# A mixture-of-experts kernel whose W1 is loaded in four column slices

## What is computed

```
t = h.reshape(B * S, -1)
probs = softmax(t @ W_gate + b_gate)
topv, topi = top_k(probs, 2)            # shares normalized to 1
mid = relu(einsum('nd,edh->neh', t, W1) + b1)     # W1: 8 x 256 x 1024
eout = einsum('neh,ehd->ned', mid, W2) + b2       # W2: 8 x 1024 x 256
out = einsum('ne,ned->nd', route, eout) @ W_out + b_out
return x + out
```

## Time and profile before

| | us |
|---|---|
| median of 3 runs | 515.55 |
| lowest, highest | 514.03, 515.56 |
| the profiled execution | 515.1 |
| its span, first to last instruction | 513.2 |
| PE busy | 494.9 |
| DVE busy | 380.6 |
| ACT busy | 283.2 |
| POOL busy | 217.5 |

### The profile page before, as it was taken

The page is one execution under the profiler, slowest core; times in us unless marked ns, Lnnn a source line. Parts: engine busy times, 40 slices in busy tenths (PEclk is TensorE's granted clock), DMA queues, the critical chain, the costliest instruction groups (busy, mean ns, idle before and its releaser), DMA issues.

```text
span 513.2 us, 14538 instructions
## 1 busy us (share of the span) xinstructions
PE 494.9 (96%) x4658; PEld 430.7 (84%) x4659; DVE 380.6 (74%) x742; ACT 283.2 (55%) x576; POOL 217.5 (42%) x264
## 2 busy tenths in 40 slices
PE   7889998899999999999999999999899999999997
PEld 7556687788888888888888888889799999998786
DVE  4789987677786776878768787676568887864675
ACT  3533544655666556665566665336668778780221
POOL 4500025048456384464844637435545453321121
PEclk9999999999999999999999999999999999999999
DMA  6406534846556464555645543433354445133983
GB/s 225 158 2 209 190 125 124 237 143 205 139 172 188 140 213 131 164 179 155 198 144 163 175 122 93 115 100 99 91 163 150 135 130 150 34 114 126 406 333 140
DMA packets 75812, 80.62 MB, mean 157 GB/s; under 512 B 42983, under 2 KB 61740, under 8 KB 74732
## 3 DMA queue, kind: packets, MB, share of 16 engines
q1 hardware_dynamic: 56912, 41.44, 26.2%
q0 software_dynamic: 7936, 22.29, 13.0%
q10 hardware_dynamic: 10908, 16.17, 9.9%
HBM read 53.40 MB, written 26.48 MB: 156 GB/s over the span
## 4 chain that ended last, share of the span: by engine, by line
PE 83%; DMA 5%; issue 5%; DVE 3%; ACT 2%; ACTq 1%; SPq 0%; another core or an unknown queue 0%; DVEq 0%
PE bank L1399 24%; PE bank L1386 10%; PE bank L1325 8%; PE bank L1326 7%; PE bank L1327 7%; PE bank L1218 5%; PE bank L1455 5%; PE bank L1372 4%; PE bank L1374 4%; PE bank L1373 4%; DMA gq<-rows_by_slot 2%; DMA w1s<-y_by_choice 1%; PE bank L1465 1%; PE bank L1188 1%; DMA brow<-in_L_ffn_b_in 1%
## 5 line engine op out<-in xcount | busy, mean ns | idle before, releaser
L713 ACT ACTIVATE region<-bank,b1p,cbits 128x256 f32<-128x256 f32 (+1 forms) x368 | 163.1, 522 | 131.9 <-PE bank L1327 51.7
L567 POOL DMA_INDIRECT y_by_choice<-region,dst x71 | 87.3, 1229 | 166.9 <-DVE region L1063 151.5
L1399 PE MATMUL bank<-w2s,region 128*128 x1200 | 136.0, 273 | 0.9 <-issue 0.7
L1399 PEld LDWEIGHTS bank<-w2s,region 128*128 128x128 f16 x1200 | 116.7, 98 | 16.7 <-issue 2.9
L1094 DVE TENSOR_TENSOR region<-region 128x512 f16<-128x512 f32 (+1 forms) x184 | 104.0, 575 | 27.7 <-ACT region L697 20.4
L1325 PE MATMUL bank<-region,w1s 128*128 128x256 f16 x384 | 104.7, 273 | 4.3 <-DVE region L1100 2.2
L1327 PE MATMUL bank<-region,w1s 128*128 128x256 f16 x384 | 104.7, 273 | 0.0
L1326 PE MATMUL bank<-region,w1s 128*128 128x256 f16 x384 | 104.7, 273 | 0.0
L559 POOL DMA_INDIRECT region<-z_by_token,src x71 | 71.9, 1013 | 75.4 <-DVE src L1020 50.6
L1090 DVE CAST region<-region 128x512 f16<-128x512 f32 x100 | 46.0, 460 | 52.1 <-ACT region L713 47.9
L1372 PE MATMUL bank<-region 128*128 128x128 f16 x336 | 57.5, 219 | 1.1 <-DVE region L1100 0.5
(11 more groups left out here) (267 smaller groups left out, 644.4 us busy)
## 6 DMA issues: line engine op xcount, KB each, us to landing
region<-in_L_ffn_W ACTq DMA_DIRECT2D x14, 1024.0 KB
rows_by_slot<-region SPq DMA_DIRECT2D x33, 256.0 KB
gq<-rows_by_slot SPq DMA_DIRECT2D x132, 64.0 KB
w1s<-y_by_choice SPq DMA_DIRECT2D x12, 512.0 KB, 11.1
w1s<-in_x SPq DMA_DIRECT2D x8, 512.0 KB, 8.3
z_by_token<-w1s SPq DMA_DIRECT2D x16, 256.0 KB, 2.1
region<-in_L_ffn_W SPq DMA_DIRECT2D x2, 1024.0 KB
region<-in_x SPq DMA_DIRECT2D x8, 256.0 KB
```

What stands on the lines that cost most here:

```text
L567: g.indirect_dma_start(out=ybuf, out_offset=bass.IndirectOffsetOnAxis(ap=at, axis=0), in_=ysb[:, a % 2, h, :], in_offset=None).then_inc(s_ ...
L713: m = s.activation(midf[:, b, c * n:(c + 1) * n], FB[b][:, c * n:(c + 1) * n], ACT.Relu, bias=b1p[:, bass.ds(r, 1), f:f + 1].rearrange("p ...
L1399: last = mm(YB[par][:, h * D:(h + 1) * D], mids[:, par, l, b, c * TS + h * P:c * TS + (h + 1) * P], w2_at(e, w, f), start=(f == 0 and l == ...
```

## The change

Both `load_w1` issue four DMAs in place of one. Each moves 256 of the 1024 columns of all 256 rows of the expert's W1, 256 KB: two runs of 1 KB per partition. Each raises `s_w1` by 16, and `w1_squares` waits for 64 per rank. Nothing else changes: same bytes, same buffer, same order of the work.

```diff
+    CW = F // 4
...
             def load_w1(j):
                 e = sp.value_load(order_i[0:1, j:j + 1], min_val=0, max_val=E - 1)
-                sp.dma_start(raw1[:], W1[bass.ds(e, 1)].rearrange("e (p k) f -> p (e k) f", p=P)).then_inc(s_w1, 16)
+                for c in range(4):
+                    sp.dma_start(raw1[:, :, c * CW:(c + 1) * CW], W1[bass.ds(e, 1), :, c * CW:(c + 1) * CW].rearrange(
+                        "e (p k) f -> p (e k) f", p=P)).then_inc(s_w1, 16)
...
             def w1_squares(j):
-                act.wait_ge(s_w1, 16 * (j + 1))
+                act.wait_ge(s_w1, 64 * (j + 1))
...
                 act.wait_ge(s_wl, 4 * j - 2)
-                act.dma_start(raw1[:], W1[bass.ds(e, 1)].rearrange("e (p k) f -> p (e k) f", p=P)).then_inc(s_w1, 16)
+                for c in range(4):
+                    act.dma_start(raw1[:, :, c * CW:(c + 1) * CW], W1[bass.ds(e, 1), :, c * CW:(c + 1) * CW].rearrange(
+                        "e (p k) f -> p (e k) f", p=P)).then_inc(s_w1, 16)
```

## The result

The changed kernel is slower: 520.6 us (519.7 to 522.1, four runs) against 515.6 (514.0 to 517.0, four runs on the same chip), a ratio of 1.010 [1.006, 1.014]. The forecast was 517.9. The profiled execution took 519.7 us with a span of 517.6, at full clock, 4.6 us more than that of before. Executions more than 1.5% above the fastest of their kernel (four in the whole series) are left out of every ratio.

What follows compares the result with a forecast made beforehand. TensorE was taken to bound the kernel; 2.4 us in the rounds plus 0.2 in the first loads gave +2.6, 517.7 us from the profiled 515.1 and 518.2 from the median. Forecast 517.9, range 515.0 to 520.6.

Steps and rivals of the forecast that it cites:

- PE bounds, and an edit is worth what it adds to PE's gaps: Whole kernel: TensorE, busy 494.9 of 513.2 us, sets the time; changes elsewhere count only by what they add to its gaps.
- Cost of three further issues, 1.86 us: ACT at the W1 load in each round: three more issues at 0.62 us, 1.86 us, bounds 1.1 and 2.4.
- The shift of the squares, 1.66 us: ACT's squares before `norms`: they move 1.66 us later, about 0.2 us of the 1.86 being lost on the way.
- PE waits at `norms` for what exceeds the room: Rounds 230, 295, 166, 133: PE loses the shift less the room, 1.44, 0.64, 0.30 and nothing, 2.4 us in sum.
- Late relus of phase 2: A round's second tile: ACT's relus start 1.86 us later, costing nothing alone, since PE needs their banks a tile later.
- First loads, +0.2 us: Second expert's loads from 86.9 us: W2 and b2 land 0.2 to 0.5 us later; +0.2 us, between -0.2 and +1.
- Transfer: W1's load: 1024 packets of 1 KB at 0.049 us, 3.1 us per DMA engine instead of 2.9, hidden in the rounds.
- SP's first load: First expert's load on SP: three more issues, some 1.5 us, covered by SP's wait of 53.6 us in z stores.
- cover: Rival in the rounds: issues overlap, cost less, or room is larger; PE loses 0 to 1 us, no change; chance 0.34.
- Faster: Rival at the first loads: 1 KB packets let bounced rows land sooner, PE's 2.19 us gap closes, 512.9 us; chance 0.08.
- Latency per part: Rival at the W1 transfer: four parts each pay their latency in turn, 8.4 us instead of 4.7, 521.0 us; chance 0.04.
- Merged packets: Rival at the W1 transfer: pieces are merged again to 8 KB, only the issues remain, 517.5 us; chance 0.03.

Runs made afterwards that it cites:

- before, second trace: The kernel before, unaltered, run again on another chip for its trace: ratio 1.0005 [0.998, 1.003].
- changed, second trace: The changed kernel, unaltered, run again on another chip against the kernel before: ratio 1.0162 [1.012, 1.020].
- slices in the rounds only: Against the kernel before, four W1 slices on ACT from the third rank on, one DMA for the first two: ratio 1.0089 [1.006, 1.012].
- ACT busy, no slices: The kernel before, one W1 DMA, with four extra reads of the expert's number on ACT behind the issue from the third rank on: 1.0107 [1.007, 1.014].
- changed, `norms` after the fourth bank: The changed kernel with every rank's `norms` after the tile's fourth bank, not the second: 1.0123 [1.008, 1.017] of the kernel before; unaltered beside it 1.0178.
- one issue, 1 KB runs: The kernel before with W1 still in one DMA but in 1 KB runs, values permuted: 507.1 us, ratio 1.0000 [0.998, 1.002].
- one further issue: W1 in two slices of 512 columns, 2 KB runs, instead of the changed kernel's four: ratio 1.0063 [1.004, 1.009] against the kernel before.
- the kernel before with late `norms`: The kernel before with `norms` after the tile's fourth bank, not the second: ratio 0.998 [0.995, 1.002].
- the kernel with the rows first: The kernel before, SP issuing the second expert's loads behind the first bounced rows, that expert's `norms` after the fourth bank: ratio 1.0003 [0.998, 1.003].

## Why the prediction was right in direction and too small

What PE lost between the first and the last `norms` of the six rounds, in us, worked out from the starts of its matmuls (what lies beyond 0.109 us between two, summed by place):

| kernel | sum | `norms`, starts of second layers | inside second layers | starts of first layers |
|---|---|---|---|---|
| before, first trace | 4.5 | 1.2 | 1.2 | 2.2 |
| before, second trace | 1.5 | 0.0 | 0 | 1.5 |
| changed, first trace | 9.2 | 2.3 | 4.4 | 2.5 |
| changed, second trace | 7.6 | 3.0 | 3.0 | 1.6 |
| slices in the rounds only | 6.0 | 4.6 | 0 | 1.4 |
| ACT busy, no slices | 7.2 | 2.6 | 1.4 | 3.3 |
| changed, `norms` after the fourth bank | 8.0 | 1.2 | 3.1 | 3.7 |
| one issue, 1 KB runs | 0.3 | 0.3 | 0 | 0 |

- **PE bounds, and an edit is worth what it adds to PE's gaps**: right, if standstills that the profile counts as busy are gaps too: with the same 4658 matmuls PE's busy time is 496.3 us (494.9 before).
- **Cost of three further issues, 1.86 us**: under-sized. By the relu behind them it is 3.60 - 1.13 = 2.47. The price was taken from b2's issue (0.47, 0.62 with its register work), but a slice has another shape, two short runs on each partition, and costs 0.55 and, from one to the next, 0.70 to 0.76; the first of the four, too, went from 0.34 to 0.55. The upper bound, 2.4, was the better value. This mis-sized term is the first of the steps that failed.
- **The shift of the squares, 1.66 us**: 2.1, from the same term. With 2.1 the prediction's own sum is 1.9 + 1.1 + 0.7 + 0.4 = 4.1 for its four rounds, and the rounds lost 6.0 - 1.3 = 4.7 in the trace. (The two rounds that it left out had 1.92 and 1.58 us of room, the latter already less than its own shift of 1.66; with them the sum is 4.8.) The agreement is luck in part, as the next point shows.
- **PE waits at `norms` for what exceeds the room**: half right. The gate holds PE's queue, in three rounds of the changed kernel's first trace and in all six of its second. But what it costs is not the shift less the room: PE goes on with what its queue had read ahead, little or nothing shows in front of `norms` (0.17 us in round 168; 0.9 us once, with slices in the rounds only; more only where W2's data itself is late), and the bill comes three to four microseconds later. In all 31 rounds of these traces in which the squares end 0.35 us or less before `norms`, the second layer behind it starts 0.26 to 0.75 us late; from 1.2 us of room on it is on time in 34 of 36 (late by 0.12 and 0.16 in the others; the kernels with `norms` after the fourth bank left out). So a gate that is only just late costs some 0.5 us a round already.
- **Late relus of phase 2, "this alone costs nothing", their banks being needed a whole tile later**: this is the main step that failed, a term put at nothing. With `norms` after the fourth bank, where the queue never waits at it, the changed kernel still lost 1.2%, of which the first loads are 0.3 (1.8% unaltered beside it), and one further issue, which moved W2's issue by 0.8 to 1.5 us, still cost 3.2 us. What the runs show in its place: ACT sits between PE's banks and DVE, and in the changed kernel it comes late to everything (first relu of the tile behind that of `norms` 4.8 to 6.4 us after the tile's start; 2.6 to 4.7 and 3.2 to 3.9 in the two traces of the kernel before). In each round of the changed kernel's two first traces one second layer, some 7 us behind the W1 issue, breaks off for 0.25 to 0.87 us (4.4 and 3.0 us in all), and first layers start late. How the late relus bring this about is argued and not shown: `norms`, powers, pieces and the next W1 issue form a loop, so a late round starts the next one late (32.7 to 33.5 us a round in the trace where PE needs 31.58), and the last paragraph of this section has what else may be in it.
- **First loads, +0.2 us, "the three extra issues there don't matter"**: the third step that failed, with a mechanism of its own. ACT waits there for b2's row, but that row is issued by ACT behind the slices, so the wait starts with them: W2's issue 2.2 us later, `norms` 1.3 us later. The kernels with slices there alone (1.0032) and in the first load but not on ACT in the rounds (1.0031) price it at 1.6 us (0.3%, interval 0.1 to 0.6%).
- **Transfer**: right (0.052 us a packet, 1.0000 with 1 KB runs). **SP's first load**: right that it is hidden; its four issues take 2.83 us and W2's issue moved from 44.12 to 46.65, a microsecond more than forecast, and PE's idle time up to 80 us did not grow.
- **Signs named beforehand**: relu 3 us behind the first issue (3.6), 12.3 us to W2's issue (12.75), packets of 0.05 us: seen. Issues 0.6 apart: 0.71. PE gaps before `norms` in rounds 166, 230 and 295: not seen as gaps; in round 166 (168 now) the queue stood there, and in the two others (235 and 301) the squares ended 1.0 and 1.2 us ahead. The gap at 97 us: it fell by 1.4 us, past the microsecond at which the prediction called itself wrong, and came back at 102.
- **Rivals**: cover fell (rounds). Faster was half right, the bounced rows did come sooner, and lost to the squares behind: in 88.3 to 91 us, where 6 packets of their queue had passed beside 99 of W1's, now 445 pass beside 477. Latency per part fell: the four slices move in 5.0 us together. Merged packets fell: 1088 packets.

**Open.** In the changed kernel's trace the instructions of PE's own queue (register arithmetic between the matmuls) stand still 17 times for 1.0 to 2.8 us between 104 and 335 us, most often for about 1.45; in the kernel with one issue and 1 KB runs never, in the kernel before 17 times in the first trace, which lost 4.5 us, and 5 times in the second, which lost 1.5. The gaps inside a second layer end with such a halt (153.23, 186.50, 218.73, 252.88), and where the queue is far ahead of the matmuls they cost nothing (the kernel before with late `norms` has nine and loses 0.6 us). The loss does not need them: with slices in the rounds only there are six, and 6.0 us are lost, 4.6 of them at `norms` and at the starts of second layers. So these halts may be what makes the gaps inside second layers, and a part of the difference between traces and chips. What stops that queue, and how much of the loss is its share, no run here tells.

## What to carry to other kernels

Before a DMA is split, price the issue on the queue that issues it, by a row of the same shape (runs for each partition, partitions), and ask what the issuing engine does next: here 256 KB slices cost 2.5 us of ACT time a round and nothing in the transfer. If an engine both feeds the bottleneck and issues DMAs, move the issue to a queue with room (SP, where the same slices were free in five rounds of six), and count every gate behind it, not only the tightest one seen in the trace. Look for the price of a late gate behind it too: the bottleneck's queue runs ahead of it, and its matmuls can stand still later than the wait, in part as busy time. The starts of the instructions show it, the busy times do not. A wait for a DMA covers nothing that is issued ahead of that DMA on the same queue.

## What the runs showed of the hardware

The time of an issue on ACT depends on its shape: 0.33 us for 32 partitions with one run each, 0.34 for 128 with one, 0.40 for 1024 runs in W2's form, 0.55 for two 1 KB runs on each of 128 partitions; the same b2 row takes 0.47 us, and 1.41 (up to 2.19 in another kernel) in the first loads, where the DMA engines are 80 to 96% busy.

How long another queue waits beside W1's depends on W1's packets: in the same 2.7 us (88.3 to 91) 6 packets of q1 passed beside 99 of q10 while W1's were of 8 KB, and with those of 1 KB in the changed kernel:

```profile
q10 hardware_dynamic: 477, 0.47, 61.7%
...
q1 hardware_dynamic: 445, 0.11, 18.1%
```

TensorE's granted clock fell to half in some executions, once behind a wait of 2.85 us in the second trace of the kernel before (98.97 us). Two windows of that trace:

```profile
98.00:102.00 4.00, 3.03 (x18) 2.19 (x19) 3.73 (x7) 2.84 (x4) 0.00 (x0) 0.72 0.34 85
102.00:106.00 4.00, 4.00 (x34) 3.35 (x32) 2.50 (x5) 1.21 (x3) 3.08 (x3) 0.85 0.56 165
```

A first-layer matmul of 256 columns goes from 0.27 to 0.42 us there and back at 103.1, that is from the 2.4 GHz level to that of 1.2 GHz for 3.4 us, which costs 1.7 us. A wait of 2.44 us in the changed kernel (102.84 us) was followed by no such fall. The clock also fell at 17 to 24 us in the kernel with the rows first. These falls are part of why runs of one kernel spread by 2 to 5 us: of twelve runs of the kernel before on one chip, the eight at full clock took 509.5 to 511.8 us and the three at 0.993 took 513.5 to 514.2.
